# Grouped layer: three of four gates projected beside the sort, group 0 kept in SBUF, TensorE two units ahead in the dense part

## The reference, cut to what matters

```
scores = softmax(LN(x) @ Wr + br)              # 4096 tokens, 64 experts
sort every expert's scores over the tokens, in groups of 64; sum each group
keep the budget of 1024 groups with the largest sums; mask the other scores
fs = kept / (kept.sum over experts + 1e-6)
y  = sum over e of fs[:, e] * ((silu(x @ Wup[e] + bup[e]) * (x @ Wgate[e] + bgate[e])) @ Wdown[e] + bdown[e])
```

## Time and profile before

| | |
|---|---|
| median of 3 runs | 2532.41 us (2529.04 to 2540.9) |
| the profiled execution's own time | 2545.23 us |
| its span | 2543.4 us |
| busy share of the span: PE, DVE, ACT, POOL | 73%, 65%, 33%, 32% |
| mean granted clock of TensorE | 0.797 of full |
| sort and search (first block of the layer) | about 1411 to 1713 us |
| second block, its start and the dense part | about 1713 to 1983 us |

### The profile page before, as it was taken

How to read it: one execution, slowest core, us unless ns; L and a number is a source line. 1 busy time by engine, 2 the same in 40 slices (tenths; PEclk the granted TensorE clock), 3 DMA queues, 4 the chain that set the end, 5 groups by cost and what they waited for, 6 DMA issues and landing times. The chain is left out here.

```text
span 2543.4 us, 47961 instructions
## 1 busy us (share of the span) xinstructions
PE 1852.9 (73%) x14115; PEld 1294.2 (51%) x14149; DVE 1643.0 (65%) x3886; ACT 835.4 (33%) x1896; POOL 808.9 (32%) x1153
## 2 busy tenths in 40 slices
PE   3999984212389987985997799217888799428883
PEld 2888872101256664653776233115666577415552
DVE  5888864689857653445676899575555477773332
ACT  1555541234444422322453577100000245202221
POOL 1555530135333233024331000002333133008884
PEclk9999995555589978996898899658999699555555
DMA  4444420000000041111003466405554000304445
GB/s 121 110 107 108 106 57 0 24 0 0 6 1 0 0 153 36 43 36 27 1 0 59 171 273 275 190 8 163 209 206 149 6 1 0 106 20 74 78 78 134
DMA packets 185139, 199.23 MB, mean 78 GB/s; under 512 B 102562, under 2 KB 164834, under 8 KB 176482
## 3 DMA queue, kind: packets, MB, share of 16 engines
q1 hardware_dynamic: 161570, 136.25, 17.6%
q10 hardware_dynamic: 9152, 47.29, 5.2%
q0 software_dynamic: 14336, 14.69, 3.4%
HBM read 106.33 MB, written 71.40 MB: 70 GB/s over the span
## 5 line engine op out<-in xcount | busy, mean ns | idle before, releaser
L2082 POOL TENSOR_TENSOR gr_tp<-gr_ring 128x512 f32<-128x512 f32 x64 | 81.9, 1280 | 491.4 <-POOLq L1835 316.6
L773 POOL TENSOR_TENSOR at_KM<-at_K,at_mask 128x512 f32<-128x512 f32 x96 | 100.0, 1041 | 309.7 <-ACT at_Q L860 309.7
L873 ACT ACTIVATE at_ET<-at_psT 128x512 f32<-128x512 f32 x192 | 114.6, 597 | 172.9 <-PE at_psT L824 172.6
L2150 PEld LDWEIGHTS gr_psY<-gr_wd,gr_h 128*128 128x128 f32 x1024 | 131.0, 193 | 69.1 <-DVE gr_h L2110 47.4
L2150 PE MATMUL gr_psY<-gr_wd,gr_h 128*128 128x128 f32 x1024 | 143.4, 283 | 25.8 <-DVE gr_h L2110 25.8
L910 DVE TENSOR_REDUCE at_mx<-at_psS 128x16 f32<-128x1024 f32 x96 | 117.6, 1225 | 61.6 <-PE at_psS L803 61.6
L249 ACT ACT_TABLE_LOAD x6 | 7.7, 1283 | 415.3 <-PEq L63 399.6
L803 PE MATMUL at_psS<-at_KM,at_Q 32*64 32x256 f32 x1536 | 135.3, 423 | 4.7 <-POOL at_KM L773 3.9
L437 POOL TENSOR_TENSOR at_E<-at_Z,at_mx 128x512 f32<-128x512 f32 x128 | 130.9, 1045 | 9.0 <-DVE at_mx L623 8.1
L824 PE MATMUL at_psT<-kept_ident,at_Z 128*128 128x128 f32 x768 | 131.6, 296 | 1.2 <-DVE at_Z L923 0.4
L2010 PE MATMUL gr_psE<-kept_xT,gr_wu 128*128 (+1 forms) x256 | 130.9, 621 | 1.6 <-ACT gr_ring L1877 1.5
(11 more groups left out here) (566 smaller groups left out, 4841.7 us busy)
## 6 DMA issues: line engine op xcount, KB each, us to landing
gr_spill<-gr_ring SPq DMA_DIRECT2D x32, 1536.0 KB, 5.1
gr_ring<-gr_spill ACTq DMA_DIRECT2D x28, 1536.0 KB, 6.5
at_amask<-mask_Bx16xSxS_ff SPq DMA_DIRECT2D x128, 128.0 KB, 2.8
at_amask<-at_amask SPq DMA_DIRECT2D x64, 256.0 KB, 3.3
gr_ring<-gr_spill SPq DMA_DIRECT2D x4, 1536.0 KB, 16.1
cap_acc<-cap_zero SPq DMA_DIRECT2D x2, 2112.0 KB, 12.5
cap_sums<-cap_acc SPq DMA_DIRECT2D x8, 512.0 KB, 7.5
ex_xs<-ex_zero SPq DMA_DIRECT2D x1, 2496.0 KB, 11.2
```

Source lines behind the costliest of these rows:

```text
L773: pool.tensor_tensor(KM[:, s, :, :], K[:, s, :].unsqueeze(1).broadcast_to([P, 4, P]), mask4[:, :].unsqueeze(2).broadcast_to([P, 4, P]), AL ...
L873: act.activation(ET[:, 4 * a:4 * a + 4, :].rearrange("p r q -> p (r q)"), psT[:, a, :], ACT.Exp, scale=QK_SCALE).then_inc(exped, 1)
L2150: last = pe.matmul(psY[:, j, :], h[:, s % 2, j * P:j * P + P], wd[:, s, :], start=False, stop=(s == C - 1), skip_group_check=True)
```

## The change

- A chunk now has seven tiles: four ups and the gates of tiles 0, 1 and 2. Only the gate of every fourth tile (s % 4 == 3) is left for the dense part.
- PE starts with group 1; the groups go 1 to 7 and then 0. Group 0 isn't stored and stays in the ring: 28 stores in place of 32, and no loads ahead of the dense part. SP's swap comes behind the stores of the seven first turns.
- The projections go through the four banks of `psV`, whose first use (the turned scores) PE now waits out (`v_taken`); unit j waits for the take of unit j - 4. `psE` is gone.
- In the dense part `psF` has four buffers, PE goes up(q + 2), down(q), and DVE has a stage `gate`, one unit ahead of `product`; `tg` has two buffers, `tp` three.
- POOL makes three products of four, and starts only when the three parts are made, since `rest` now shares its memory with `tp` and `tg` (`work`).

```diff
-        CHUNKS, TILES = 4, 6
+        CHUNKS, TILES = 4, 7
-        kind_of = [(0, True), (0, False), (1, True), (2, True), (2, False), (3, True)]
+        kind_of = [(0, True), (0, False), (1, True), (1, False), (2, True), (2, False), (3, True)]
...
-                    spill_group(0)
                     with sp.Fori(1, GROUPS2) as g:
-                        spill_group(g)
+                        for u in range(CHUNKS):
+                            sp.wait_ge(taken, CHUNKS * TILES * (g - 1) + TILES * (u + 1))
+                            sp.dma_start(spilled_to(CHUNKS * g + u), slot_of(u)).then_inc(spilled[u], 16)
                     sp.wait_ge(swapped, 1)
...
                     for u in range(CHUNKS):
-                        sp.wait_ge(spilled[u], 16 * GROUPS2)
-                        sp.dma_start(slot_of(u), spilled_to(u)).then_inc(back[u], 16)
+                        sp.wait_ge(spilled[u], 16 * (GROUPS2 - 1))
...
+                    pe.wait_ge(v_taken, 1)
...
-                            wait_past(pe, taken, CHUNKS * TILES * g + j - 1)
-                            pe.matmul(psE[:, j % 2, :], w, x, start=True, stop=True).then_inc(multiplied, 1)
+                            wait_past(pe, taken, CHUNKS * TILES * turn + j - 3)
+                            pe.matmul(psV[:, j % 4, :], w, x, start=True, stop=True).then_inc(multiplied, 1)
+                    multiply_group(0, 1)
+                    with pe.Fori(1, GROUPS2 - 1) as turn:
+                        multiply_group(turn, turn + 1)
+                    multiply_group(GROUPS2 - 1, 0)
...
+            work = sb("work", [P, 7, 512], on=second)
+            rest = work[:, 0:4, :].rearrange("p a b -> p (a b)")
+            tp, tg, h = work[:, 0:3, :], work[:, 3:5, :], work[:, 5:7, :]
+            psG, psF = pb("psG", [P, 2, 512], on=second), pb("psF", [P, 4, 512], on=second)
...
                     def product(q, s, g):              # POOL
-                        if s % 2:
+                        if s % 4 == 3:
                             return
-                        pool.wait_ge(back[s // 4], 16 * (g + 1))
+                        wait_past(pool, back[s // 4], 16 * g)
                         wait_past(pool, h_ready, q - 3)
+                    pool.wait_ge(part_ready, 3)
...
+                    def gate(q, s, g):                 # DVE; the copy of fs at s == 0 stands here too
+                        if s % 4 == 3:
+                            dve.wait_ge(up_ready, q + 1)
+                            wait_past(dve, back[s // 4], 16 * g)
+                            wait_past(dve, h_ready, q - 3)
+                            dve.scalar_tensor_tensor(tg[:, s // 4 % 2, :], psG[:, s // 4 % 2, :], bg[:, s:s + 1], ring[:, s // 4, WAITING, :],
+                                                     ALU.add, ALU.mult).then_inc(gated, 1)
-                    run(dve, [(0, product), (-1, residual), (-2, measure)])
+                    run(dve, [(1, gate), (0, product), (-1, residual), (-2, measure)])
...
                     def up(q, s, g):
-                        wait_past(pe, h_ready, q - 1)
+                        wait_past(pe, h_ready, q - 3)
-                        if s % 2:
+                        if s % 4 == 3:
...
-                    run(pe, [(0, up), (-1, down)])
+                    run(pe, [(2, up), (0, down)])
```

More of the change, by code:

```diff
@@ L1867, in _, with take_group @@
                     act.wait_ge(w_loaded, 16 * 6)
-                    def take_group(g):
+                    def take_group(turn):
                         for j in range(CHUNKS * TILES):
@@ L1872, in take_group @@
                             c = 4 * u + k
-                            act.wait_ge(multiplied, CHUNKS * TILES * g + j + 1)
+                            act.wait_ge(multiplied, CHUNKS * TILES * turn + j + 1)
                             if j % TILES == 0:
-                                wait_past(act, spilled[u], 16 * g)
+                                wait_past(act, spilled[u], 16 * turn)
                             bias = bu[:, c:c + 1] if is_up else bg[:, c:c + 1]
-                            act.activation(ring[:, u, j % TILES, :], psE[:, j % 2, :], ACT.Silu if is_up else ACT.Identity, bias=bias).then_inc(taken, 1)
+                            act.activation(ring[:, u, j % TILES, :], psV[:, j % 4, :], ACT.Silu if is_up else ACT.Identity, bias=bias).then_inc(taken, 1)
                     take_group(0)
-                    with act.Fori(1, GROUPS2) as g:
-                        take_group(g)
+                    with act.Fori(1, GROUPS2) as turn:
+                        take_group(turn)
                 @block.vector
@@ L2001, in _, with multiply_group @@
                     pe.wait_ge(w_loaded, 16 * 6)
-                    def multiply_group(g):
+                    pe.wait_ge(v_taken, 1)
+                    def multiply_group(turn, g):
                         x = m.xT[:, bass.ds(512 * g, 512)]
@@ L2029, in _ @@
                     pe.wait_ge(kept, 1)
+                    pe.wait_ge(taken, CHUNKS * TILES * GROUPS2)
                     for b in range(4):
@@ L2099, in product @@
                             dve.tensor_scalar(fst[:, :], fs[:, bass.ds(512 * g, 512)], 1.0, None, ALU.mult).then_inc(staged, 1)
-                        dve.wait_ge(up_ready, q + 1)
-                        if s % 2:
[L2102 to L2105, removed]
+                        if s % 4 == 3:
[4 more added lines that the diff above has]
+                                                     ALU.add, ALU.mult).then_inc(gated, 1)
+                    def product(q, s, g):
+                        dve.wait_ge(up_ready, q + 1)
+                        if s % 4 == 3:
+                            dve.wait_ge(gated, ones_of(s, g))
                         else:
-                            dve.wait_ge(pooled, pairs(s, g))
+                            dve.wait_ge(pooled, threes(s, g))
                         wait_past(dve, down_done, q - 1)
-                        product_of = tg[:, :] if s % 2 else tp[:, s // 2 % 2, :]
-                        dve.tensor_tensor(h[:, s % 2, :], psF[:, s % 2, :], product_of, ALU.mult).then_inc(h_ready, 1)
+                        product_of = tg[:, s // 4 % 2, :] if s % 4 == 3 else tp[:, s % 4, :]
+                        dve.tensor_tensor(h[:, s % 2, :], psF[:, s % 4, :], product_of, ALU.mult).then_inc(h_ready, 1)
                     def residual(q, s, g):
```

38 lines of the change are left out of this document (15 added, 23 removed).

## The result

The changed kernel takes 2477.64 us (median of 4 runs, 2473.39 to 2480.2) where the kernel before took 2535.22 (4 runs): a ratio of 0.9771, 95% interval 0.9746 to 0.9796. That is 57.6 us less. Forecast were 59.1 us less, 2473 us, with a range of 2450 to 2500.

A forecast was written before the change was run, and what follows sets the result against it. The first block was taken as bound by the projections through two buffers, the dense part by PE's work plus waits for DVE. Terms of -15.1, -2.0 and -42.0 summed to -59.1 us, giving 2473 us, range 2450 to 2500.

The forecast's parts named there:

- The one stall of four units: Dense part: PE waits 0.62 us for DVE once in four units, as the gate of unit 3 stands before product 2.
- the dense part: Third term: groups of 25.9 us against 31.0, the first 30.7 against 37.0; -42.0 us over the eight.
- The 4.8 us lost at half clock: First group of the dense part: about 9.6 us at half speed, the same loss assumed after the change.
- The eighth turn of the projections: Group 0's projections on PE until 1610, hidden before the search's first count at about 1619, 9 us to spare.
- Term 1: Sort stage: with four buffers takes go at PE's pace, 0.854 us, and the swap goes out earlier; -15.1 us.
- The turn: Change of groups in the dense part: PE stalls 0.72 us for X += psY, and bdown takes 1.08.
- term 2: Start of the second block: POOL waits for the parts, so DVE's casts get shorter and PE starts earlier; -2.0 us.
- more stalls: Rival, dense part: a second unit of four waits for DVE, 28.8 us a group, 2496 us; 20 in 100.
- no gain beside the sort: Rival, sort stage: the pace stays 0.95, bound by the store or ACT, 2492 us; 6 in 100.
- loads that bind: Rival, dense part: POOL and DVE wait for larger ring loads; at 9.4 us a chunk 2554 us; 4 in 100.
- No stall in the dense part: Rival: DVE far enough ahead that the gate never holds product 2; 23.0 us a group, 2450 us; 12 in 100.
- The rival of the copy of fs: Dense part: DVE's copy of fs waits out one POOL product, eight times 1.3, 10 us, 2483 us; 3 in 100.

The follow-up runs named there:

- two_banks: The changed kernel with two banks of psV in use for the projections instead of four; 2480.6 us, 0.985 of the kernel before on its chip.
- banks_alone: The kernel before with four banks of psV for the projections instead of two of psE, nothing else; 2499.4 us, 0.9928 of the kernel before.
- pool_early: The changed kernel with POOL free to start beside DVE's casts, rest lying over tg and h, without waiting for the parts; 2467.77 us, one run.
- lower_first: The changed kernel with the second block's first DMAs reordered, fs and parts of the lower half of the tokens ahead; 0.9768 of the kernel before.
- lead_one: The changed kernel with PE one unit ahead instead of two, up(q + 1), down(q); 2505.0 us, 0.988 of the kernel before on its chip.
- gate_behind: The changed kernel with DVE's list as product, gate instead of gate, product; 2451.05 us, 0.9674 of the kernel before on its chip.
- swap_first: The changed kernel with the swap of the halves ahead of the last of the 28 stores on SP; 0.9744 of the kernel before on its chip.

## Why the prediction was right

**Where it was right.** The reading that the first block was bound by the projections and not by the sort, and that two banks held them, is shown from both sides by two_banks and banks_alone. The one stall of four units, at tile s % 4 == 2 and because of the gate's place in DVE's list, is in the trace, and it goes when the gate goes behind; its size was 0.5 us for 0.62. A group of 25.9 us was forecast and 25.9 measured, the dense part -44.1 us for -42.0: the next seven groups -36.5 for -35.7, the first -7.6 for -6.3. The 4.8 us lost at half clock were taken over from the kernel before, and there the first 9.7 us of the dense part ran at the lower level (1727.93 to 1737.62); in the changed kernel it was 6.5 us (1710.42 to 1716.95), 1.6 us less lost:

```profile
1710.00:1742.00 32.00, 29.60 (x180) 23.13 (x181) 16.31 (x28) 0.00 (x0) 17.70 (x14) 0.89 0.62 225
```

That is 0.89 over 32 us for 0.85. The eighth turn of the projections, the larger stores and loads, POOL's third product and the copy of fs cost nothing that shows.

**What was mis-sized.** Term 1, -15.1, was -13.4 at DVE's resumption. A product takes 0.858 us and not 0.854 (196 x 0.004 = 0.7), the start at half clock cost some 0.5 more, and the swap took 10.2 us for 9.9 behind the larger store. The stall behind the gate was 0.12 too large, because h of tile 2 doesn't read what the gate writes: it starts 0.67 us after the gate and not 0.79, as in the row I took it from. Four such stalls make a group 0.5 us shorter than forecast. The turn made it as much longer: PE waited 0.96 us for 0.72 (its psF ends at 1764.60, bdown starts at 1765.56; the 0.81 in brackets leaves out the way through the array), the first gate's stall behind the turn was 0.17 longer than the others, and the first down, behind a stall, took 1.0 for 0.89. That a group came out at the 25.9 us of the forecast to the tenth is luck.

**The step that failed** is term 2: "The parts' DMAs and PE's start hang on them", on DVE's casts. The casts became 2.0 us shorter as said, and nothing came of it. SP's issues for the twelve parts took 9.47 us before and 10.47 after, ending 11.9 and 11.8 us after the first copy, and from the first copy to PE it was 14.55 and 14.56. The row before:

```profile
1715.79 9.47 SPq L2064 DMA_DIRECT2D gr_parts<-gr_part  x12
```

Over all runs with the twelve copies ahead of PE it was 14.55 to 15.29. Pool_early made the casts 3 us longer with the same start, and lower_first, with half of the copies ahead of PE, started it 4.5 us sooner. The queue of copies was the path. The trace of before had the twelve issues going on for 2.6 us after the third part was made (1722.6 to 1725.26), and I read the wait for the DMA as a wait for its last input.

The rivals that kept their chance without coming true: more stalls (lead_one shows what they would look like, at 30.6 us a group), no gain beside the sort, loads that bind. "No stall in the dense part" was 2450 us; gate_behind is that kernel, and ran in 2451 on a chip where the kernel before takes 7 us less.

## What to carry to other kernels

Follow the waiting order through the steady state by hand, with start-to-start distances from the trace: an engine's list decides the stall, and one stage written ahead of another cost 19 us here. When an engine runs ahead by n units, ask which operation the lead is for; the plain units here got nothing from it. And before an input of a DMA is made faster, see whether the queue in front of the waiting engine is full: shorten what must land first.

## What the runs showed of the hardware that was not expected

The start of PE's projections differs by execution. After 2.06 us without work PE's halves of a product were 0.85 us apart until 1416.6 in the changed kernel, which is its lower level, 1.2 GHz; in pool_early, with the same code up to there, the third product begins 1.80 us after the first, the upper level from the start. The granted clock is 0.55 from 1413 to 1417 in the changed kernel, and 1.00 from 1406 to 1410 in pool_early:

```profile
1406.45 1.10 PE L2006 MATMUL gr_psV<-kept_xT,gr_wu 128*128 128x512 f32 x2 [2.06 <-ACT gr_V L1860]
...
1408.25 1.02 PE L2006 MATMUL gr_psV<-kept_xT,gr_wu 128*128 128x512 f32 x2
```

```profile
1413.08 2.04 PE L2006 MATMUL gr_psV<-kept_xT,gr_wu 128*128 128x512 f32 x2 [2.06 <-ACT gr_V L1860]
...
1416.61 1.02 PE L2006 MATMUL gr_psV<-kept_xT,gr_wu 128*128 128x512 f32 x2
```

The first of these is pool_early, the second the changed kernel. The third product stands 3.53 us behind the first there, 1.73 more, and the swap goes out at 173.67 for 171.94, 1.73 later. A stage that is bound by PE inherits this; differences of that size between two runs here are not the edits'.

In pool_early POOL's products beside DVE lengthened a cast from 1.23 to 2.33 us and a subtraction of two SBUF tensors from 2.29 to 3.23. In the dense part of the changed kernel, where DVE reads one operand from PSUM, 15.3 us of POOL's work in 26 left h at 0.685 us. This is what "SBUF — State Buffer" of the Trainium skill, section "SBUF: two separate sides", says of the shared port pair: DVE operations with two SBUF inputs or in a two-port mode contend with POOL for it, the others don't.

The rival of the copy of fs named a mechanism that exists, at another place. In gate_behind the first copy waited for its own DMA, came while POOL was at work, and took 1.02 us for the usual 0.41; in swap_first it took 1.05 and in two_banks 1.51:

```profile
1697.67 3.88 POOL L2082 TENSOR_TENSOR gr_work<-gr_ring 128x512 f32<-128x512 f32 x3 [310.79 <-DVE gr_part L2094]
1699.41 1.02 DVE L2101 TENSOR_SCALAR gr_fst<-gr_fs 64x512 f32<-64x512 f32 x1 [1.81 <-DMA gr_fs<-gr_V]
```

PE started 5.3 us after that copy ended, so it cost nothing. At the turns of groups DVE is first, as the prediction said. In the changed kernel the copy takes 0.41 us there, and it is POOL's product, 0.17 us behind, that takes 1.38 for 1.27:

```profile
1762.13 0.41 DVE L2101 TENSOR_SCALAR gr_fst<-gr_fs 64x512 f32<-64x512 f32 x1
1762.30 1.38 POOL L2082 TENSOR_TENSOR gr_work<-gr_ring 128x512 f32<-128x512 f32 x1 [1.37 <-DVE gr_work L2117]
```
